# Regrouping the token-shift mixes and the query tail in the second layer's first stage (two-layer recurrent network, eight cores)

## What is computed

```python
xn = _layernorm(x)                                   # x after layer 0
q, k, v = split(xn @ W_qkv.T)                        # attention, no heads
s = softmax(q @ k.T / 32) @ v
x_prev = concat([zeros, xn[:, :-1]])                 # shifted by one token
xr = mu_r * xn + (1 - mu_r) * x_prev
xk = mu_k * xn + (1 - mu_k) * x_prev
g = silu(sigmoid(xr @ W_r.T) * (square(relu(xk @ W_k.T)) @ W_v.T))
x = x + s * g
```

## Time and profile before

| | us |
|---|---|
| median of two runs | 1571.65 |
| the two runs | 1549.07, 1594.24 |
| the profiled execution, whole | 1549.27 |
| its slowest core, core 3, first to last instruction | 1548.2 |
| the other cores' spans | 1537.6 to 1547.9 |

### The profile page before, as it was taken

The page is one execution under the profiler, slowest core; times in us unless marked ns, Lnnn a source line. Parts: engine busy times, 40 slices in busy tenths (PEclk is TensorE's granted clock), DMA queues, the critical chain, the costliest instruction groups (busy, mean ns, idle before and its releaser), DMA issues.

```text
span 1548.2 us, 16588 instructions; the slowest of 8 cores (1537.6 to 1548.2 us)
## 1 busy us (share of the span) xinstructions
PE 1278.8 (83%) x6016; PEld 576.0 (37%) x6016; DVE 553.7 (36%) x527; ACT 307.0 (20%) x356; POOL 140.6 (9%) x236
## 2 busy tenths in 40 slices
PE   0587889999999999997135879889899878888886
PEld 0233334444444444443012333333344434444443
DVE  0614231001111136455387742132333434444443
ACT  1222311011111132332112445222200011111110
POOL 0001111011111100001000000000000101111111
PEclk9799999999999999999567999999999999999998
DMA  8333334246544545642723333633221204333322
GB/s 178 103 61 55 55 57 80 41 74 103 82 72 79 118 95 126 169 125 74 178 85 106 92 71 69 164 69 68 62 38 31 62 17 102 93 89 82 82 76 61
DMA packets 74159, 133.29 MB, mean 86 GB/s; under 512 B 23904, under 2 KB 32096, under 8 KB 72032
## 3 DMA queue, kind: packets, MB, share of 16 engines
q0 software_dynamic: 32384, 77.61, 28.5%
q1 hardware_dynamic: 33632, 42.03, 8.4%
q10 hardware_dynamic: 8064, 12.59, 2.3%
HBM read 159.47 MB, written 29.36 MB: 122 GB/s over the span
## 4 chain that ended last, share of the span: by engine, by line
PE 71%; DVE 16%; ACT 5%; issue 3%; DMA 3%; DVEq 1%; SPq 0%; ACTq 0%; POOL 0%; POOLq 0%
PE psf L347 10%; PE psf L353 10%; DVE BP L145 9%; PE psf L940 8%; PE psf L964 7%; PE psf L827 7%; PE psf L468 7%; DVE FP L145 7%; PE psf L386 5%; PE psf L438 5%; ACT BP L145 4%; PE psf L675 2%; PE psf L754 2%; PE psf L766 2%; PE psf L211 1%
## 5 line engine op out<-in xcount | busy, mean ns | idle before, releaser
L145 ACT ACTIVATE BP<-psf 128x512 bf16<-128x512 f32 (+1 forms) x192 | 128.3, 668 | 516.7 <-PE psf L353 305.6
L347 PE MATMUL psf<-BP 128*128 128x512 bf16 x768 | 187.7, 389 | 28.9 <-DVE BP L145 27.2
L145 DVE TENSOR_TENSOR BP<-BP,psf 128x512 bf16<-128x512 bf16 x96 | 66.0, 687 | 370.2 <-ACT BP L145 369.5
L353 PE MATMUL psf<-BP 128*128 128x512 bf16 x768 | 182.6, 381 | 0.0
L211 PE MATMUL psf<-BP,ones 128*128 128x512 bf16 x64 | 34.8, 544 | 116.7 <-ACT BP L145 104.6
L940 PE MATMUL psf<-BP 128*128 128x512 bf16 x512 | 121.5, 398 | 1.3 <-DVE BP L145 1.2
L347 PEld LDWEIGHTS psf<-BP 128*128 128x128 bf16 x768 | 75.8, 99 | 125.2 <-issue 39.3
L964 PE MATMUL psf<-BP 128*128 128x512 bf16 x512 | 115.5, 385 | 2.4 <-DVE BP L145 2.4
L827 PE MATMUL psf<-BP 128*128 128x512 bf16 x512 | 113.5, 383 | 3.8 <-DVE FP L145 3.8
L468 PE MATMUL psf<-BP 128*128 128x512 bf16 x512 | 111.8, 379 | 0.0
L353 PEld LDWEIGHTS psf<-BP 128*128 128x128 bf16 x768 | 75.6, 98 | 92.5 <-issue 3.4
(11 more groups left out here) (66 smaller groups left out, 1111.3 us busy)
## 6 DMA issues: line engine op xcount, KB each, us to landing
BP<-wg POOLq DMA_DIRECT2D x48, 256.0 KB, 3.7
BP<-wu POOLq DMA_DIRECT2D x48, 256.0 KB, 4.5
BP<-wd POOLq DMA_DIRECT2D x16, 768.0 KB, 7.9
FP<-xt SPq DMA_DIRECT2D x32, 256.0 KB, 7.9
FP<-xt SPq DMA_DIRECT2D x8, 1024.0 KB, 9.4
x1s<-FP SPq DMA_DIRECT2D x8, 1024.0 KB, 7.2
FP<-x1s SPq DMA_DIRECT2D x32, 256.0 KB, 7.0
FP<-x1s POOLq DMA_DIRECT2D x16, 512.0 KB, 6.7
```

Of the source, the lines that this page charges most:

```text
L145: ins = fn(*a, **k)
L347: te.matmul(pg, lhsT, rhs, start=(k == 0), stop=(k == NCH - 1))
L353: ins = te.matmul(pu, lhsT, rhs, start=(k == 0), stop=(k == NCH - 1))
```

## The change

The mixes of spans 1 and 2 are each issued later, the tail of the span-1 queries is issued one step earlier (after CSMM(2), no longer after EP(2)), and the first four key units of half 0 are issued after AFN(2) and the queries of span 2 (they came before AFN(2)). No operation is added or removed.

```diff
-        def post11():
-            q_tail(1)
+        def post12():
+            mixes(1)
+            q_block(2)
             for o in range(4):
                 k_unit(0, o)
 
         def post15():
+            mixes(2)
             mixes(3)
             q_block(3)
             for o in range(NCH):
                 k_unit(1, o)
 
         post = {5: lambda: (mixes(0), q_mma(0)), 7: lambda: q_tail(0),
-                8: lambda: (mixes(1), bcol_save(), q_mma(1)), 11: post11,
-                12: lambda: (mixes(2), q_block(2)),
+                8: lambda: (bcol_save(), q_mma(1)), 10: lambda: q_tail(1),
+                12: post12,
                 14: lambda: [k_unit(0, o) for o in range(4, NCH)],
                 15: post15}
```

## The result

The changed kernel is slower: 1.0157 times the kernel before, with a 95% interval of 1.0146 to 1.0169, so about +24.3 us on 1550; its median over all runs is 1575.82 us. Forecast were +22.7 us and 1572. The change is under 2%, and the prediction said that a measurement of this kernel can hardly tell such a one from none; the interval, 1.0146 at its lower end, tells it plainly.

The account below looks back on a forecast made before the run. PE sets the pace (71% of the chain), but in the changed stage the chain hops between engines; half 1's start moves 20.9 us, plus 1.8 cold restart: 1549.3 + 22.7 = 1572 us, range 1564 (also given as 1563) to 1584.

Parts of the forecast that it names:

- Step 1: CSMM(2) on PE starts at 830.8 instead of 840.27, 9.5 us won; its 16 matmuls take 3.6 us.
- 2 q_tail(1) through, EP(2) starts: q_tail(1), now ahead of EP(2): matmuls end at 842.5, drains at 847.7; EP(2) on DVE starts at 842.7.
- 3 Ln, AFN(2): Ln of EP(2) stands on ACT behind q_tail(1)'s drains, at 847.8; AFN(2) at 849.4, where it was 850.74.
- 4 mixes(1) begins: On DVE after AFN(2)'s 9.06 us: mixes(1) from 858.5 to 876.4, with q_block(2) hidden under it on PE.
- 5 key units 0 to 3: Key units wait for mixes(1), start at 876.7, take 15.0 us on PE; ACT is through at 893.2.
- step 6: Squares wait on ACT behind the key units; CSMM(3) at 897.3, cold; EP(3) at 903.6, 4.7 us earlier.
- 7 mixes(2), mixes(3), half 1's keys: Behind AFN(3): mixes(2) from 916.7 takes 25.61 us, mixes(3) 18.24; half 1's keys at 960.5, +20.9 us.
- 8 restart cold: Half 1's first 32 matmuls on PE run cold after 26 us of idle: +1.8 us.
- head start: The 9.5 us by which CSMM(2) starts earlier; only 1.3 us of it forecast to be left at AFN(2).
- second rival: EP(2)'s Ln and Exp run right after CSMM(2), later steps 10.7 us earlier: +12.0, 1561 us; chance 0.06.
- third rival: Not slower: late mixes covered, as if mixes(2) gets into DVE's idle stretch; 1545 us, chance 0.03.
- The upper bound: If CSMM(2), q_tail(1) and key units 0 to 3 all run cold, with a longer restart: +29.3 us, 1.9%.

Follow-up runs that it names:

- e1: Changed kernel with mixes(2) alone moved from behind AFN(3) to after CSMM(3), in DVE's idle stretch; 0.999 of the kernel before.
- my own version: Changed kernel reordered statistics first, with q_tail(1) behind EP(2) and mixes(2) behind CSMM(3)'s cast; 0.9995 of the kernel before.
- the kernel with both mended: Changed kernel with mixes(2) moved to after CSMM(3) and q_tail(1) put back behind EP(2); 0.9913 of the kernel before, median 1537.95 us.

## Why the prediction was right

| step of the prediction | forecast | changed kernel, core 0 |
|---|---|---|
| 1 CSMM(2) on PE | 830.8 | 833.12 |
| 2 q_tail(1) through, EP(2) starts | 842.7 | 845.05 |
| 3 Ln, AFN(2) | 847.8, 849.4 | 850.13, 851.75 |
| 4 mixes(1) begins | 858.5 | 860.81 |
| 5 key units 0 to 3 | 876.7 | 879.04 |
| 6 CSMM(3), EP(3) | 897.3, 903.6 | 899.73, 905.34 |
| 7 mixes(2), mixes(3), half 1's keys | 916.7, 942.3, 960.5 | 918.46, 943.88, 961.98 |
| 8 restart cold | +1.8 | +1.6 |

The mechanism is shown, not only read: mixes(2) into the gap takes the loss away, mixes(2) late by itself brings it, half of it brings 0.0069 of the 0.0167 that lie between e1 and the changed kernel. So is the second half of the argument, that q_tail(1) eats the head start: 9 us come back when it is moved, and the prediction's second rival is in effect that kernel (forecast 1561, measured 1.0097, so some 1565). What the third rival needed, mixes(2) in DVE's idle stretch, is what e1 does by hand (forecast 1545, measured 0.999, so some 1548).

The pieces' prices held to 0.2 us: mixes(1) 17.97 us (860.81 to 878.78), mixes(2) 25.42, mixes(3) with the handing over 18.10. What was off is the step in front. Step 1 took the squares of CSMM(2) where they were, at 826.81. On core 0 they ran at 829.14: of the two drains before them the first waited 4.34 us for an earlier store of queries. Before, such a delay was harmless, for CSMM(2) waited until 840.02 for the cast; in the changed kernel the squares end last, and 2.3 us go straight down to step 6. There 0.7 come back, for CSMM(3) to EP(3) took 5.61 us, not 6.27, and 0.3 in the mixes. So half 1 starts 22.4 us later than before and not 20.9.

Core 0 hides a second slip. Its PE had idled only 0.70 us ahead of CSMM(2), so it doesn't test the 3.6 us that step 1 took for 16 matmuls after 2.6 us of idle. On core 2, the slowest of this trace (1572.2 us), the squares ran at 826.81 and CSMM(2) started at 830.78, both as forecast, but the 16 matmuls took 5.30 us, and EP(2) started at 844.39, 1.7 late. Of the six cores of this trace that idled 2.38 to 2.57 us there, five were slow (5.2 to 5.3 us) and one fast (3.61). The prediction's ground for 3.6, that 2.6 us is less than half of any idle that slow matmuls followed, doesn't hold on its own rows: half of 4.96 is 2.5. And the trace of before has a shorter one, behind the rows that it shows:

```profile
974.75 8.75 PE L754 MATMUL psf<-BP 128*128 128x512 bf16 x32 [3.51 <-DMA BP<-wr]
```

The upper bound allows for the slow case. That the sum is off by no more than 1.6 us (24.3 against 22.7) is in part luck: on core 0 one slip of some 2 us came in, on core 2 the other, on neither both. (The lower end of its range stands once as 1564 and once as 1563; nothing hangs on that.)

The sum, on these two cores: 22.4 to the start of half 1; 1.6 for the restart (971.53 - 961.98 = 9.55, against 947.54 - 939.62 = 7.92; 1.3 of it are slower matmuls, 8.42 against 7.07, and 0.3 is the wait behind them, here for a `wk` load); 0.6 more from there to the loop over `wv` and `wr` (27.79 against 27.21: longer waits for `wk` loads, a shorter one for `wr`); 0.7 less behind it (572.8 against 573.5). Together 23.9, the difference of the spans 1572.1 and 1548.2. The forecast had 22.7.

The order on DVE held where it was put to the test: mixes(2) was ready and didn't pass the waiting EP(3), in 24.27 us of idle here and in 46.87 where mixes(2) was moved alone.

## What to carry to other kernels

Work that nothing waits for yet still has a place: the gap it lies in. Before moving a block off the chain, ask which gap it will take, what lay there, and what that block will then stand in front of; here 18 us went from ahead of CSMM(2)'s cast, which started AFN(2) no earlier (851.75 against 850.74), and 25.6 us came to stand ahead of half 1's keys. A wait written as "the semaphore's count so far" and an in-order engine's queue both tie a step to all that is written ahead of it, so look at every engine that the step uses: EP(2) was held on DVE and on ACT, and mending DVE alone, as I did in my own version, moved the stall to ACT and PE.

## What the runs showed of the hardware that was not expected

The prediction found no row for the clock that PE has after 2.6 us of idle, and took the fast one. It isn't one answer. PE of the changed kernel on core 2, CSMM(2), 2.57 us after the queries:

```profile
830.78 0.38 PE L211 MATMUL psf<-BP,ones 128*128 128x512 bf16 x1 [2.57 <-ACT BP L145]
...
831.42 0.38 PE L213 MATMUL psf<-BP,ones 128*128 128x512 bf16 x1
831.64 0.55 PE L211 MATMUL psf<-BP,ones 128*128 128x512 bf16 x1
831.98 0.63 PE L213 MATMUL psf<-BP,ones 128*128 128x512 bf16 x1
...
834.97 0.46 PE L211 MATMUL psf<-BP,ones 128*128 128x512 bf16 x1
835.27 0.38 PE L213 MATMUL psf<-BP,ones 128*128 128x512 bf16 x1
```

The first five start 0.215 us apart; from 831.98 to 834.97 are seven gaps of 0.43; then it is fast again. The granted clock of the three stretches, in the windows (columns as in the earlier trace rows), shows the two levels, 2.4 and 1.2 GHz (1.00, and near 0.5 in the middle one, whose ends take in some fast matmuls):

```profile
830.70:831.60 0.90, 0.82 (x4) 0.42 (x5) 0.00 (x0) 0.00 (x0) 0.00 (x0) 1.00 1.07 394
831.60:835.30 3.70, 3.70 (x11) 1.34 (x10) 0.00 (x0) 0.00 (x0) 0.00 (x0) 0.54 0.33 123
835.30:836.10 0.80, 0.78 (x4) 0.17 (x2) 0.00 (x0) 0.00 (x0) 0.00 (x0) 1.00 0.00 0
```

The clock fell while PE was working, after the idle was over, and the 16 matmuls took 5.3 us. In the kernel with both mended, core 3, the same 16 came after 2.42 us of idle and were all fast, through in 3.6 us (829.95 to 833.56):

```profile
829.95 0.38 PE L211 MATMUL psf<-BP,ones 128*128 128x512 bf16 x1 [2.42 <-ACT BP L145]
```

The length of the idle doesn't decide it either: in the trace of the changed kernel core 6 was fast after 2.56 us (3.61 us for the 16) and core 3 slow after 2.38 (5.30). A short idle of PE near 2.5 us is thus worth 0 or some 1.7 us in these runs, and a first fast matmul doesn't tell which.
